# A decoder layer on one core: the end rewritten with a transposed down projection

## The chip, the cores and the metric

The kernel runs on one core of a Trainium2 chip. TensorE multiplies into PSUM (eight banks of 128 x 512 floats), VectorE and ScalarE read PSUM and SBUF, GpSimd reads SBUF alone, and SyncE (SP) only issues transfers. The engines run side by side and wait for each other by semaphores. The metric is the device time of one execution in microseconds (us); less is better.

## The reference

One decoder layer on x (1024 tokens of 128) with a context of 6404 tokens. Three parts, each followed by a residual and a layer norm:

```python
x = _layernorm(x + attn(x, U))                       # softmax of -dist^2 of x @ U
x = _layernorm(x + xattn(ctx, ctx, x, Wq, ..., Wo, bo))   # 16 heads of depth 8, 6404 keys
x = _layernorm(x + ffn(x, clip_x, clip_down, w_gate, w_up, w_down))

def ffn(x, ...):                                     # inner width 352
    xq = act_fake_quant(x, clip_x)      # one scale for the whole tensor:
                                        # sigmoid(clip) * max|x| / 127, round, clip to [-128, 127]
    gate = xq @ weight_fake_quant(w_gate).T          # one scale per row of a weight
    up = xq @ weight_fake_quant(w_up).T
    h = act_fake_quant(silu(gate) * up, clip_down)   # again one scale for the whole tensor
    return h @ weight_fake_quant(w_down).T
```

Both activation scales need the largest value of a whole tensor before the next step can begin.

## The kernel before

Everything is hand-scheduled: every engine has its own program, and the order of its instructions and its waits is written out. Until about 72 us the first attention runs, beside the projection of keys and values and the rounding of the feed-forward weights on VectorE (`ffn_weights`, seven parts between other work). Then comes the loop over `PHASES` = 8 phases (4 groups of heads by 2 halves of the queries) of 17 chunks of 384 keys: TensorE makes scores (line 1404) three banks at a time, ScalarE takes their exponential (line 768), VectorE takes one unit of most chunks over with a polynomial (lines 1055 to 1088, with GpSimd at line 641), and TensorE multiplies by the values (line 1434) into two accumulator banks. In most phases `add_acc`, `turn_acc` and four transfers bring the divided result to `o_t` while the next phase runs. The loop ends at 743.4 us with the last exponentials.

The end is one serial stretch:

- TensorE projects the first half of the queries by `wo_sb` (`project_out(0)`, line 1518), and multiplies the last values. VectorE adds `x1_bo` (line 1120) and takes the statistics (line 834).
- Last phase: VectorE copies and adds the accumulators (lines 1041, 1042), TensorE transposes them (1532), VectorE takes a reciprocal of 16 columns (1129) and multiplies (1131), TensorE turns it back (1551), ScalarE copies it into `o_t` (789), TensorE projects the second half. In between, TensorE transposes the rounded weights (1541, 1546), spreads `dn_diag`, the scale of the down rows (1536), and VectorE copies all that (1138, 1142, 1147).
- Second layer norm: moments (840), square root on ScalarE (803), reciprocal and shift (1153, 1154), five rows of 128 tokens on VectorE (845) and three on ScalarE (797). A tile of "row j" holds 128 tokens by 128 columns.
- First scale: the largest of x2 (1173), transposed into one row (1569), reduced (1165), spread by a matmul with `ones_row` (1571), multiplied by the clip (1168), reciprocal (1170).
- x2 is transposed (1564), scaled and rounded by adding `ROUND` (808, 1178), and clipped into `xq_t` (1180 to 1187).
- Three tiles of the inner width (128, 128, 96 rows), each over all 1024 tokens: gate and up (1584, into four banks), silu on ScalarE (815), product (1195) and its largest value (1200) on VectorE.
- Second scale in the same way, then h is scaled and rounded (VectorE 1206, ScalarE 821) and clipped (1211, 1213) into `hq`.
- Down (1596): `hq` is the stationary operand, 24 matmuls of 128 columns. Its result stands with tokens on the partitions; VectorE multiplies it by the scales (1220), adds x2 (1225), and takes the statistics; then the third norm and two output transfers, five rows by SP (553) and three by ScalarE (828).

`zeros_into` (line 1237) issues matmuls of zeros between the steps. `Chain.step` makes an engine wait for its own instruction. GpSimd has nothing to do in the end.

Of the kernel before, what the change touches and what calls it, by code (L numbers as in the profile page):

```python
# [23 lines left out]
BF16 = mybir.dt.bfloat16  # L24
# [19 lines left out]
G = 4  # L44
# [16 lines left out]
DVE_ROWS = 5  # L61
# [32 lines left out]
def decoder_layer(nc, x, ctx_in, U, Wq, bq, Wk, bk, Wv, bv, Wo, bo, clip_x, clip_down,  # L94
                  w_gate, w_up, w_down, out, score_limit=SCORE_LIMIT):
    stack = ExitStack()
    with stack:
# [20 lines left out]
        ones_row = sb("ones_row", [1, P])  # L118
        minus_sel = sb("minus_sel", [P, 1])
        eps_col = sb("eps_col", [P, 1])  # L120
        round_col = sb("round_col", [P, 1])
        last_rows = sb("last_rows", [P, G])
# [56 lines left out]
        last_rden = sb("last_rden", [P, 4, G])  # L179
        last_att = sb("last_att", [P, 4, G, DH])  # L180
# [14 lines left out]
        dn_diag = sb("dn_diag", [P, D])  # L195
        ones_sq = sb("ones_sq", [P, P])
        dn_bc = sb("dn_bc", [P, D])
        gmax = sb("gmax", [P, 8])
        gmax_row = sb("gmax_row", [1, 2])
        act_s = sb("act_s", [P, 8])  # L200
        gu_s = sb("gu_s", [P, 2, IT])
# [11 lines left out]
        x2_t = attn_e[:, 2 * IT, :]  # L213

# [43 lines left out]
        pe_tail, dve_tail, act_tail = sem("pe_tail"), sem("dve_tail"), sem("act_tail")  # L258
# [173 lines left out]
        def _(sp):  # L432
# [90 lines left out]
            all_written()  # L523
            for ph in range(PHASES):
# [27 lines left out]
            sp.wait_ge(dve_tail, TAIL_OUT)  # L552
            sp.dma_start(out_rows[:, 0:DVE_ROWS, :], res[:, 0:DVE_ROWS, :]).then_inc(out_written, 16)
# [5 lines left out]
        def _(pool):  # L559
# [5 lines left out]
            pool.memset(round_col[:], ROUND)  # L565
            chain.step(pool.memset(last_rows[:], 1.0))
# [20 lines left out]
            pool.memset(v_all[:, :, :, DH:DH + 1], 1.0)  # L587

# [12 lines left out]
            pool.memset(ones_row[:], 1.0)  # L601
# [42 lines left out]
            for ph in range(PHASES):  # L644
                for c in range(NC):
                    m = ph * NC + c
                    stage(m % 2, m, c * CT, ph % NG * G)
                    if c != 1 and c < NC - 1:
                        powers(ph, c)


        @block.scalar
        def _(act):
# [121 lines left out]
            for ph in range(PHASES):  # L775
# [8 lines left out]
                for s in range((NC - 1) * BPC, BPP):  # L784
# [3 lines left out]
            act.wait_ge(pe_tail, TAIL_ATT_T)  # L788
            act.activation(o_t[32 * (NG - 1):P, HQ:T], ps[32 * (NG - 1):P, 1, :], ACT.Copy
                           ).then_inc(act_tail, 1)  # L790
            act.preload_act_table(ACT.Sqrt)

            def norm(signal, target):

                act.wait_ge(dve_tail, signal)
                for j in range(DVE_ROWS, TQ):
                    last = act.activation(target[:, j, :], res[:, j, :], ACT.Identity,
                                          scale=rstd[:, j:j + 1], bias=shift[:, j:j + 1])
                return last


            act.wait_ge(dve_tail, TAIL_VAR2)
            act.activation(rstd[:], mean_var[:, :, 1], ACT.Sqrt, bias=eps_col[:]).then_inc(act_tail, 1)
            norm(TAIL_NORM2, x2).then_inc(act_tail, 1)
            act.preload_act_table(ACT.Silu)

            act.wait_ge(dve_tail, TAIL_S2)
            act.activation(x2_t[:, HQ:T], ps[:, 1, :], ACT.Identity, scale=act_s[:, 1:2],
                           bias=round_col[:]).then_inc(act_tail, 1)
            for rows, a, b in ISPANS:  # L810
                for i in range(a, b):
                    act.wait_ge(pe_tail, TAIL_GU + 2 * i)
                    act.wait_ge(dve_tail, TAIL_XQ)
                    bank = 4 * (i % 2)
                    act.activation(silu[0:rows, i, :], ps[0:rows, bank:bank + 2, :], ACT.Silu,
                                   scale=gu_s[0:rows, 0, i:i + 1]).then_inc(act_tail, 1)
            act.preload_act_table(ACT.Sqrt)

            act.wait_ge(dve_tail, TAIL_S3)
            for rows, i in ((P, 1), (I - 2 * P, 2)):  # L820
                act.activation(h_f[0:rows, i, :], h_f[0:rows, i, :], ACT.Identity,
                               scale=act_s[0:rows, 3:4], bias=round_col[0:rows, :]).then_inc(act_tail, 1)

            act.wait_ge(dve_tail, TAIL_VAR3)
            act.activation(rstd[:], mean_var[:, :, 1], ACT.Sqrt, bias=eps_col[:]).then_inc(act_tail, 1)
            norm(TAIL_NORM3, res).then_inc(act_tail, 1)
            act.wait_ge(act_tail, ACT_OUT)
            act.dma_start(out_rows[:, DVE_ROWS:TQ, :], res[:, DVE_ROWS:TQ, :]).then_inc(out_written, 16)


        def spread(dve, js):

            for j in js:
                last = dve.bn_stats(stats[:, j, :], res[:, j, :])  # L834
            return last

        def moments(dve):

            for j in range(TQ):
                last = dve.bn_aggr(mean_var[:, j, :], stats[:, j, :])  # L840
            return last

        def normalise(dve, target, js):
            for j in js:
                last = dve.tensor_scalar(target[:, j, :], res[:, j, :], mean_var[:, j, 0:1],
                                         rstd[:, j:j + 1], ALU.subtract, ALU.mult)
            return last

        @block.vector
        def _(dve):  # L850
# [52 lines left out]
            def ffn_weights(part):  # L903
# [24 lines left out]
                elif part == 4:  # L928
                    for w, _, q in each:
                        last = dve.tensor_scalar(q, w, ROUND, None, ALU.subtract)  # L930
                    dve.tensor_scalar(dn_diag[:], ident[:], w_dn_s[:, 1:2], None, ALU.mult)
# [712 lines left out]
```

## Time and profile before

| | us |
|---|---|
| runs shown, median (lowest to highest) | 790.36 (789.95 to 790.44) |
| the profiled execution | 790.35 |
| its span | 788.6 |
| busy: PE / ScalarE / VectorE / GpSimd | 702.3 / 723.9 / 602.8 / 176.3 |
| granted TensorE clock, mean of the span | 0.993 |

The profile shows one execution. Its span is from the first to the last recorded event, and the device time has a little around it. Times in the rows are counted from the span's start. A chain of work is followed back from the last instruction, at each step to what released it. The granted clock is 1.00 at 2.4 GHz and 0.50 at 1.2 GHz. A float matmul is recorded as two passes, each with a weight load.

### The profile page before, as it was taken

To read this page: it belongs to the slowest core of one execution; us is meant where nothing else is said; L and a number is where in the kernel's file an instruction comes from. 1 tells how busy PE (TensorE), PEld (TensorE's weight loads), DVE (VectorE), ACT (ScalarE), POOL (GpSimd) and SP (SyncE) were. 2 spreads that over 40 slices of the span, in tenths; PEclk is the share of its full clock that TensorE was granted. 3 is DMA by queue.
4 is the path that set the end of the run, shared out by engine and by line. 5 is a ranking of instruction groups with operands and counts; after the bars stand their busy time and mean duration, and the time that the engine had idled before them with its cause. 6 is when DMAs were issued, how large, how long until landed. Compare 5 with 4: busy or idle time off the path is not lost.

```text
span 788.6 us, 36646 instructions
## 1 busy us (share of the span) xinstructions
PE 702.3 (89%) x15159; PEld 312.5 (40%) x15163; DVE 602.8 (76%) x1709; ACT 723.9 (92%) x632; POOL 176.3 (22%) x318
## 2 busy tenths in 40 slices
PE   9998999989999999989999999899999999899864
PEld 5464344334443344334433443344334443444332
DVE  4668688768886888678867887788868886788676
ACT  4477999999999999999999999999999999999751
POOL 4437122212221222122221222122212221222100
PEclk9999999999999999999999999999999999999997
DMA  4364111111111111111111111111111111111000
GB/s 139 119 178 158 41 45 36 37 44 43 36 37 43 45 39 36 41 44 41 35 40 45 42 35 40 45 42 36 36 45 45 37 36 42 39 34 37 4 1 27
DMA packets 36980, 38.35 MB, mean 49 GB/s; under 512 B 8936, under 2 KB 35466, under 8 KB 36884
## 3 DMA queue, kind: packets, MB, share of 16 engines
q1 hardware_dynamic: 35776, 36.57, 15.9%
q8 instruction: 65, 1.06, 0.5%
q10 hardware_dynamic: 1108, 0.46, 0.2%
q14 instruction: 31, 0.25, 0.1%
HBM read 30.12 MB, written 6.42 MB: 46 GB/s over the span
## 4 chain that ended last, share of the span: by engine, by line
ACT 58%; issue 26%; PE 11%; DVE 3%; ACTq 1%; DVEq 0%
ACT probs L768 57%; PE ps L1311 2%; PE ps L1237 1%; PE ps L1264 1%; PE ps L1272 1%; PE ps L1302 1%; PE ps L1434 1%; PE ps L1255 1%; PE ps L1404 1%; ACTq L781 1%; ACTq L766 0%; DVE stats L834 0%; DVE probs L1195 0%; PE ps L1518 0%; PE ps L1353 0%
## 5 line engine op out<-in xcount | busy, mean ns | idle before, releaser
L768 ACT ACTIVATE probs<-ps 128x1536 f32<-128x1536 f32 (+1 forms) x536 | 669.3, 1393 | 2.0 <-PE ps L1404 2.0
L1434 PE MATMUL ps<-probs,v_op 64*9 64x512 f32 (+1 forms) x8256 | 522.8, 496 | 0.0
L1404 PE MATMUL ps<-q_op,k_op 59*32 59x512 bf16 x6432 | 332.5, 379 | 63.0 <-ACT probs L768 60.7
L1404 PEld LDWEIGHTS ps<-q_op,k_op 59*32 59x32 bf16 x6432 | 101.6, 89 | 347.8 <-issue 259.1
L1055 DVE TENSOR_SCALAR e_t<-ps 128x256 f32<-128x256 f32 x240 | 90.8, 420 | 142.7 <-PE ps L1404 142.7
L1434 PEld LDWEIGHTS ps<-probs,v_op 64*9 64x9 f32 x8256 | 171.3, 86 | 62.2 <-issue 4.2
L641 POOL TENSOR_SCALAR e_pow<-e_t 128x512 int32<-128x512 int16 x120 | 74.3, 619 | 356.0 <-DVE e_t L1055 356.0
L634 POOL COPY v_op<-v_all 128x108 f32<-128x108 f32 x136 | 64.4, 474 | 168.3 <-PE ps L1434 167.8
L1083 DVE SCALAR_TENSOR_TENSOR e_f<-e_f,e_pow 128x256 f32<-128x256 f32 x240 | 98.8, 450 | 0.0
L1077 DVE SCALAR_TENSOR_TENSOR e_f<-e_u,e_f 128x256 f32<-128x256 f32 x240 | 90.6, 419 | 0.0
L1072 DVE SCALAR_TENSOR_TENSOR e_u<-e_f 128x256 f32<-128x256 f32 x240 | 90.3, 418 | 0.2
L1088 DVE SCALAR_TENSOR_TENSOR probs<-e_u,e_f 128x256 f32<-128x256 f32 x240 | 89.7, 412 | 0.0
L1061 DVE SCALAR_TENSOR_TENSOR e_f<-ps,e_t 128x256 f32<-128x256 f32 x240 | 89.6, 415 | 0.0
L704 ACT ACTIVATE probs<-ps,neg_n 128x1024 f32<-128x1024 f32 x8 | 8.9, 1113 | 18.9 <-PE ps L1302 18.9
L1237 PE MATMUL ps<-zeros_bf 128*128 128x512 bf16 x79 | 22.4, 427 | 3.1 <-DVE probs L1195 1.4
L883 DVE SCALAR_TENSOR_TENSOR probs<-ps,bias_cols,k_parts 128x384 f32<-128x384 f32 x17 | 10.5, 616 | 17.7 <-ACT k_parts L690 10.3
L594 POOL TENSOR_TENSOR k_parts<-probs,k_parts 128x384 bf16<-128x384 f32 x17 | 15.5, 912 | 1.4
L1264 PE MATMUL ps<-ctx_t,wk_turned 128*128 128x384 f32 x34 | 14.8, 518 | 0.7 <-DVE probs L883 0.7
L592 POOL CAST k_parts<-probs 128x384 bf16<-128x384 f32 x17 | 8.5, 503 | 30.1 <-DVE probs L883 29.9
L1311 PE MATMUL ps<-probs,x_nat 128*128 128x512 f32 x32 | 15.1, 593 | 0.0
L1272 PEld LDWEIGHTS ps<-wv_sb,ctx_t 128*128 128x128 f32 x102 | 13.6, 191 | 3.4 <-issue 0.5
L1272 PE MATMUL ps<-wv_sb,ctx_t 128*128 128x128 f32 x102 | 14.0, 275 | 0.0
(186 smaller groups left out, 244.9 us busy)
## 6 DMA issues: line engine op xcount, KB each, us to landing
k_op<-k_parts_dram SPq DMA_DIRECT2D x544, 36.0 KB
k_parts_dram<-k_parts SPq DMA_DIRECT2D x17, 288.0 KB, 2.9
k_op<-k_parts_dram SPq DMA_DIRECT2D x272, 12.0 KB
ctx_nat<-in_ctx_dram SPq DMA_DIRECT2D x16, 192.0 KB, 3.2
q_op<-q_parts_dram SPq DMA_DIRECT2D x32, 48.0 KB
q_parts_dram<-q_parts SPq DMA_DIRECT2D x2, 384.0 KB, 3.5
x_nat<-in_x_dram SPq DMA_DIRECT2D x1, 512.0 KB, 3.6
o_t<-att_rows SPq DMA_DIRECT2D x28, 16.0 KB
```

Of the source, the lines that this page charges most:

```text
L634: pool.tensor_copy(v_op[:, slot].rearrange("p j (h d) -> p j h d", h=G), v_all[:, bass.ds(tile, CT), head:head + G, :]).then_inc(v_staged, 1)
L641: pool.tensor_scalar(e_pow[:], e_low(e_t[:]), float(2 ** 23), float(EXP2_LEAD), ALU.mult, ALU.add).then_inc(e_pow_ready, 1)
L768: act.activation(probs[:, b % NP].rearrange("p u t -> p (u t)")[:, 0:columns], ps[:, bank:bank + BU, :].rearrange("p u t -> p (u t)")[:, 0 ...
L1055: dve.tensor_scalar(e_t[:, cols], score, E_MIN, ROUND + EXP2_OFF, ALU.max, ALU.add).then_inc(e_step, 1)
L1061: dve.scalar_tensor_tensor(out=e_f[:, cols], in0=score, scalar=E_MIN, in1=e_low(e_t[:, cols]), op0=ALU.max, op1=ALU.subtract).then_inc(e_s ...
L1072: dve.scalar_tensor_tensor(out=e_u[:, cols], in0=e_f[:, cols], scalar=a, in1=e_f[:, cols], op0=ALU.add, op1=ALU.mult).then_inc(e_step, 1)
L1077: dve.scalar_tensor_tensor(out=e_f[:, cols], in0=e_u[:, cols], scalar=d, in1=e_f[:, cols], op0=ALU.add, op1=ALU.mult).then_inc(e_step, 1)
L1083: dve.scalar_tensor_tensor(out=e_f[:, cols], in0=e_f[:, cols], scalar=e, in1=e_pow[:, cols].bitcast(F32), op0=ALU.add, op1=ALU.mult).then_ ...
L1088: dve.scalar_tensor_tensor(out=probs[:, block % NP, BU - 1, 512 - EW + cols.start:512 - EW + cols.stop], in0=e_u[:, cols], scalar=b, in1=e ...
L1272: last = pe.matmul(ps[:, v_bank(n), P * j:P * j + P], ctx_t[:, n % 3, P * j:P * j + P], wv_sb[:], start=True, stop=True)
L1404: return pe.matmul(ps[a:a + P // G, bank, :], k_op[W2 * r:W2 * r + KR, kslot, i, P * j + a:P * j + a + P // G], q_op[W2 * r:W2 * r + KR, q ...
L1434: last = pe.matmul(ps[32 * k:32 * k + DH + 1, ACC[h], a:b], v_op[W2 * h:W2 * h + W2, slot, j, (DH + 1) * k:(DH + 1) * (k + 1)], probs[W2 * ...
```

## The change

- Entry of the loop: TensorE transposes the rounded weights before it reads the flag; VectorE copies them there (`w_t_made`, `w_t_copied`), and TensorE's second score block waits for that. SP loads rows of Wo into `wo_pad` with four more transfers. GpSimd makes `den_sel`, a matrix that spreads the denominators.
- Last phase: no transposes. ScalarE copies half an accumulator, VectorE adds the other, TensorE spreads the denominators over the partitions with `den_sel`, VectorE takes a reciprocal of [128 x 256] and multiplies, twice. The projection accumulates x1 + bo (`added`), the older heads, and the last ones through `wo_pad`, in PSUM.
- The second norm runs in parts: rows 0 to 3 early, 4 and 5, then 6 and 7, with values read from PSUM.
- The scale: the largest values are put on a diagonal with the clip, a matmul with `ones_sq` spreads them, and one reduce takes the largest.
- Feed-forward: six units of 512 tokens instead of three of 1024; VectorE makes all six products and their largest values. `gu_s` is made by GpSimd.
- Rounding h: tile 0 on VectorE, tile 1 on ScalarE, tile 2 on GpSimd, the clipping mostly on VectorE, in halves.
- Down: the weights are the stationary operand, nine matmuls in three column groups (`DOWN`); the result stands transposed, is scaled into `o_s` per partition, and TensorE turns it back onto x2, which stands in PSUM already.
- The third norm reads PSUM; ScalarE takes rows 0 to 3 and VectorE 4 to 7, with a transfer of 256 KB each.

The diff, cut to its core:

```diff
+            pool.wait_ge(scale_ready, 1)
+            for rows, a, b in ISPANS:
+                pool.tensor_scalar(gu_s[0:rows, :, a:b], w_gu_scale[0:rows, :, a:b],
+                                   act_s[0:rows, 0:1], None, ALU.mult).then_inc(gu_s_ready, 1)
+            pool.wait_ge(scale_ready, 2)
+            rows = FFN_ROWS[2]
+            for half in range(2):
+                cols = slice(HQ * half, HQ * half + HQ)
+                chain.step(pool.tensor_scalar(h_f[0:rows, 2, cols], h_f[0:rows, 2, cols],
+                                              act_s[0:rows, 3:4], ROUND, ALU.mult, ALU.add))
+                pool.tensor_scalar(hq[0:rows, 2, cols], h_f[0:rows, 2, cols], ROUND, QMAX,
+                                   ALU.subtract, ALU.min).then_inc(h_pool, 1)
...
+            for half in range(2):
+                cols = slice(EH * half, EH * half + EH)
+                act.activation(acc_sb[:, cols], ps[:, ACC[0], cols], ACT.Copy).then_inc(acc_copied, 1)
...
+                chain.step(act.activation(h_f[:, 1, cols], h_f[:, 1, cols], ACT.Identity,
+                                          scale=act_s[:, 3:4], bias=round_col[:]))
+                act.activation(hq[:, 1, cols], h_f[:, 1, cols], ACT.Identity, bias=unround_col[:]
+                               ).then_inc(h_act, 1)
...
+            for half, cols in enumerate(halves):
+                dve.wait_ge(den_spread, half + 1)
+                dve.wait_ge(acc_summed, half + 1)
+                chain.step(dve.reciprocal(rden[:, cols], ps[:, half, 0:EH]))
+                dve.tensor_tensor(att[:, cols], acc_sb[:, cols], rden[:, cols], ALU.mult
+                                  ).then_inc(att_scaled, 1)
...
+            def on_diagonal(n, column, clip):
+                dve.tensor_scalar(diag[:, n, :], ident[:], gmax[:, column:column + 1],
+                                  sig[:, clip:clip + 1], ALU.mult, ALU.mult).then_inc(diag_ready, 1)
...
+            for u, (i, half, rows) in enumerate(FFN_UNITS):
+                cols = slice(HQ * half, HQ * half + HQ)
+                dve.wait_ge(gu_done, 2 * u + 2)
+                dve.wait_ge(silu_ready, u + 1)
+                dve.scalar_tensor_tensor(
+                    out=h_f[0:rows, i, cols], in0=ps[0:rows, FFN_BANKS[u][1], :],
+                    scalar=gu_s[0:rows, 1, i:i + 1], in1=silu[0:rows, i, cols],
+                    op0=ALU.mult, op1=ALU.mult).then_inc(h_ready, 1)
+                dve.wait_ge(h_ready, u + 1)
+                last = largest_of(u)
...
             pe.wait_ge(bo_ready, 1)
+            wt = ps[:, 4, :].bitcast(BF16)
...
+            last.then_inc(w_t_made, 1)
             pe.wait_ge(flag_ready, 1)
             with pe.If(pe.value_load(flag[0:1, 0:1]) > 0):
...
+            pe.wait_ge(h_ready, 4)
+            added(0, x2[:, 0:4, :], 4)
+            added(1, x2[:, 4:6, :], 2)
+            added(5, x2[:, 6:8, :], 2)
+            zeros_into(7, 8)
+            spread_max(2, 0)
+            zeros_into(6, 9)
+            for n, (bank, a, b) in enumerate(DOWN):
+                pe.wait_ge(hq_ready, a // HQ + 1)
+                for i, rows in enumerate(FFN_ROWS):
+                    last = pe.matmul(ps[:, bank, 0:b - a], w_dn_t[0:rows, i, :], hq[0:rows, i, a:b],
+                                     start=(i == 0), stop=(i == IT - 1))
+                last.then_inc(down_done, 1)
...
+FFN_UNITS = [(i, half, FFN_ROWS[i]) for half in range(2) for i in range(IT)]
+FFN_BANKS = [(2, 3), (4, 6), (7, 0), (1, 5), (2, 3), (4, 6)]
+DOWN = [(2, 0, HQ), (3, HQ, HQ + EH), (4, HQ + EH, T)]
```

## Rows read from the trace of the kernel before

**Rows 1.** The page, chain that ended last, share of the span by line.
```profile
ACT probs L768 57%; PE ps L1311 2%; PE ps L1237 1%; PE ps L1264 1%; PE ps L1272 1%; PE ps L1302 1%; PE ps L1434 1%; PE ps L1255 1%; PE ps L1404 1%; ACTq L781 1%; ACTq L766 0%; DVE stats L834 0%; DVE probs L1195 0%; PE ps L1518 0%; PE ps L1353 0%
```

**Rows 2.** The chain in order of time, 743 us on: start, us, what.
```profile
743.39 2.73 PE ps L1434 x40
...
759.19 0.76 DVE probs L1178
...
763.39 1.29 DVE probs L1195
...
772.95 0.76 DVE probs L1206
...
777.06 0.87 PE ps L1596 x12
...
779.47 0.87 DVE stats L834 x4
...
782.66 0.65 DVE mean_var L840 x8
...
784.11 1.26 ACT res L797 x3
```

**Rows 3.** Timeline of ScalarE's queue, its last row: start, us, engine, line, operation.
```profile
785.40 0.37 ACTq L828 DMA_DIRECT2D out_dram<-res  x1
```

**Rows 4.** Groups by line and form, ScalarE: count | busy us, mean ns | idle.
```profile
L815 ACT ACTIVATE probs<-ps,gu_s 128x1024 f32<-128x1024 f32 x2 | 2.1, 1111 | 2.2 <-PE ps L1584 2.2
...
L665 ACT ACTIVATE x_t<-ps 128x512 f32<-128x512 f32 x1 | 0.6, 597 | 1.5 <-PE ps L1246 1.5
```

**Rows 5.** Groups by line and form, VectorE, wide operations.
```profile
L1055 DVE TENSOR_SCALAR e_t<-ps 128x256 f32<-128x256 f32 x240 | 90.8, 420 | 142.7 <-PE ps L1404 142.7
...
L1195 DVE SCALAR_TENSOR_TENSOR probs<-ps,gu_s,probs 128x1024 f32<-128x1024 f32 x2 | 2.6, 1280 | 1.9 <-ACT probs L815 1.9
...
L1220 DVE SCALAR_TENSOR_TENSOR res<-ps,act_s,dn_bc 128x512 f32<-128x512 f32 x2 | 1.5, 744 | 1.0 <-PE ps L1596 1.0
...
L992 DVE TENSOR_REDUCE q_abs<-q_parts 128x1 f32<-128x512 bf16 x2 | 1.3, 672 | 0.0
```

**Rows 6.** TensorE: a group by form, and a row of the chain.
```profile
L1311 PE MATMUL ps<-probs,x_nat 128*128 128x512 f32 x32 | 15.1, 593 | 0.0
...
750.75 1.17 PE ps L1518 x8
```

**Rows 7.** Groups by line and form, VectorE, reciprocals.
```profile
L1095 DVE RECIPROCAL att_rden<-acc_t 128x16 f32<-128x16 f32 x7 | 1.8, 254 | 0.2
L1153 DVE RECIPROCAL rstd<-rstd 128x8 f32<-128x8 f32 x2 | 0.4, 203 | 0.4 <-ACT rstd L825 0.4
...
L948 DVE RECIPROCAL attn_rden<-attn_den 128x8 f32<-128x8 f32 x1 | 0.2, 193 | 0.0
```

**Rows 8.** Line 922 on VectorE (ns min/median/max), and GpSimd's timeline at that time.
```profile
L922 DVE TENSOR_SCALAR w_gu<-w_gu,w_gu_inv x6: 273/274/798, 30.0 to 31.5; 128x128 f32<-128x128 f32 x4, 96x128 f32<-96x128 f32 x2
...
29.81 0.91 POOL L594 TENSOR_TENSOR k_parts<-probs,k_parts 128x384 bf16<-128x384 f32 x1
```

**Rows 9.** Groups by line and form, GpSimd, tensor_scalar.
```profile
L641 POOL TENSOR_SCALAR e_pow<-e_t 128x512 int32<-128x512 int16 x120 | 74.3, 619 | 356.0 <-DVE e_t L1055 356.0
...
L574 POOL TENSOR_SCALAR wq_sb<-wq_sb 128x128 f32<-128x128 f32 x1 | 0.5, 522 | 0.0
```

**Rows 10.** Stretches of 1 us: PE, PEld, DVE, ACT, POOL busy (count), PEclk, DMA.
```profile
767.00:768.00 1.00, 0.82 (x2) 0.28 (x3) 0.96 (x2) 0.81 (x1) 0.00 (x0) 0.57 0.00 0
...
770.00:771.00 1.00, 1.00 (x5) 0.35 (x3) 0.96 (x2) 0.00 (x0) 0.00 (x0) 0.72 0.00 0
```

**Rows 11.** Timelines of TensorE, VectorE and SP at the loop's entry.
```profile
73.13 0.61 PE L1404 MATMUL ps<-q_op,k_op 59*32 59x512 bf16 x12 [1.46 <-issue]
...
76.60 0.76 DVE L1055 TENSOR_SCALAR e_t<-ps 128x256 f32<-128x256 f32 x2 [2.99 <-PE ps L1404]
...
79.52 4.71 SPq L331 DMA_DIRECT2D k_op<-k_parts_dram  x6
```

More of the change, by code:

```diff
@@ L833, in spread, with moments @@
+            last.then_inc(out_act, 1)
+            act.wait_ge(out_act, 1)
+            act.dma_start(out_rows[:, 0:HALF, :], res[:, 0:HALF, :]).then_inc(out_written, 16)
+        def spread(dve, tiles):
+            for j, tile in tiles:
+                last = dve.bn_stats(stats[:, j, :], tile)
+            return last
+        def moments(dve, js):
             for j in js:
[L834 to L839, printed above, removed]
@@ L965, in _ @@
             dve.wait_ge(res_ready, 2)
-            chain.step(spread(dve, range(TQ)))
-            moments(dve).then_inc(var_ready, 1)
+            chain.step(spread(dve, res_rows(range(TQ))))
+            moments(dve, range(TQ)).then_inc(var_ready, 1)
             dve.wait_ge(std_ready, 1)
@@ L1227, in _, with inverse @@
-            chain.step(last)
-            moments(dve).then_inc(dve_tail, 1)
-            norm(ACT_STD3, res)
+            dve.wait_ge(res_projected, 1)
+            chain.step(dve.tensor_tensor(res[:, 0:HALF, :].rearrange("p j d -> p (j d)"), ps[:, 2, :],
+                                         x1_bo[:, 0:HALF, :].rearrange("p j d -> p (j d)"), ALU.add))
+            chain.step(spread(dve, res_rows(range(HALF))))
+            moments(dve, range(HALF)).then_inc(ln_var, 1)
+            def inverse(js, std, count):
+                dve.wait_ge(std, count)
+                chain.step(dve.reciprocal(rstd[:, js], rstd[:, js]))
@@ new lines, in _ @@
+            for half, cols in enumerate(halves):
+                dve.wait_ge(den_spread, half + 1)
[3 more added lines that the diff above has]
+                                  ).then_inc(att_scaled, 1)
+            dve.wait_ge(res_projected, 2)
+            chain.step(spread(dve, bank_rows(3, (4, 5))))
+            moments(dve, (4, 5)).then_inc(ln_var, 1)
@@ new lines, in _ @@
+            pe.wait_ge(x1_bo_ready, 1)
+            added(3, x1_bo[:, 4:6, :], 2)
+            added(4, x1_bo[:, 6:8, :], 2)
+            pe.wait_ge(den_sel_ready, 1)
+            for half in range(2):
+                pe.wait_ge(acc_summed, half + 1)
+                pe.matmul(ps[:, half, 0:EH], den_sel[:].rearrange("p k i -> p (k i)"),
+                          acc_sb[:, EH * half:EH * half + EH], start=True, stop=True).then_inc(den_spread, 1)
+            pe.wait_ge(o_written, 16 * G * (PHASES - 1))
@@ new lines, in _ @@
+            pe.wait_ge(wo_pad_loaded, 16 * G)
+            for half in range(2):
+                rows = [(ps[:, 3 + half, P * n:P * n + P], EH * half + P * n) for n in range(2)]
+                for to, a in rows:
+                    pe.matmul(to, o_t[0:D - 32, HQ + a:HQ + a + P], wo_sb[0:D - 32, :], start=False,
+                              stop=False, skip_group_check=True)
+                pe.wait_ge(att_scaled, half + 1)
+                for to, a in rows:
+                    last = pe.matmul(to, att[:, a:a + P], wo_pad[:], start=False, stop=True,
+                                     skip_group_check=True)
+                last.then_inc(res_projected, 1)
@@ L1604 @@
+            turned_back(5, (6, 7))
 W_LOADS = 16 * 5
```

472 lines of the change are left out of this document (251 added, 221 removed).

## The prediction

> **What bounds the kernel now.** I read the page first, and there the chain that ended last: 57% of the span is ScalarE's exponentials [rows 1]. That loop isn't touched, so only two stretches can move: the entry of the loop near 72 us, and the end. The chain in order of time gives the end as one line of steps, each waiting for the one ahead [rows 2]: TensorE's last values end at 746.12, the first activation scale is used at 759.19, the first silu times up starts at 763.39, the second scale is used at 772.95, the down projection starts at 777.06 and the last rows are normalised from 784.11. The output transfer is issued at 785.40 [rows 3]. Of 788.6 us of span, 42.5 us is this serial end, in which no engine is full; its price is the sum of latencies on whichever engine has the baton, mostly VectorE. The profiled execution took 790.35 us, its span 788.6 and 1.75 us around it; the median shown is 790.36, so a shift in the span can be taken from the median directly. 0.2% is 1.6 us, about what a measurement of this kernel can tell from no change.
>
> **The change part by part.** I write the new end out with durations of like instructions, 0.03 us for a hop between engines, and compare at the milestones of [rows 2].
>
> *Attention's last division.* Before: copy, add, four transposes, a 16-wide reciprocal, a multiply, four matmuls, a copy, the projection; the second half of the residual is complete only at 752. New: ScalarE copies 256 columns (0.38 us: 597 ns for 512 [rows 4], less some 0.9 ns a column), VectorE adds 256 (0.42, as the 256-wide PSUM form [rows 5]), TensorE spreads denominators (256 float columns in two passes; a pass of 512 is 15.1/32 = 0.47 [rows 6], so some 0.6 with the latency). It has two `added` matmuls ahead, 0.94, and can start only at 747.0. The reciprocal starts at 747.6. It is now 256 wide, twice. No such width is in the trace. At 8 and 16 columns it took 203 and 254 ns [rows 7], 6.3 ns a further column, while other operations pay about 1 (1280 ns against 744 for 1024 against 512 [rows 5]). Lower bound: 0.42, as any 256-wide operation; upper bound 16 times the 16-wide one, 4.1. I take 254 + 240 x 6.3 = 1.75 us, the slope of the nearest rows. With a 0.42 multiply behind each, both halves are done at 752.0, so this move alone wins nothing.
> The Trainium skill ("VectorE: DVE Perf Modes", the section on the pipe's eight slices) gives the reciprocal an iterative divide with a repeat count of 8. At the 0.96 GHz that the skill gives VectorE that is an estimate of 8.3 ns a column, 2.25 us each, and the sum would be 1.0 us later; the trace's own increments are lower.
>
> *Second layer norm and first scale.* After 752.0 VectorE does stats and moments of rows 4, 5 (0.7: four stats take 0.87, eight moments 0.65 [rows 2]), the largest of half of x2 (0.69, from 672 [rows 5]), a diagonal (0.27), stats and moments of rows 6, 7 (0.7), two tiny ops (0.4), ScalarE two rows (0.87, by three in 1.26 [rows 2]), the other largest (0.69), diagonal (0.27), a spread matmul (0.4), a reduce of 256 (0.42), a reciprocal (0.16), hops 0.3, less 0.3 of overlap. Sum 5.6: the scale is ready at 757.6 against 759.2, gain 1.6. The old route through one row, a matmul and a multiply goes away.
>
> *Quantised x.* The scale to the first half's xq: ScalarE 0.5, VectorE 0.43 and 0.3, with hops 1.4. Then one matmul (0.4), a silu of 512 (0.66: 1111 ns for 1024 [rows 4], less 512 x 0.9), hops: the first silu times up starts at 760.15 against 763.39, gain 3.2. gu_s moved to GpSimd, two tiny ops under 0.6 us of others' work; uncovered they would cost 0.4. The weight copies and the transposes that stood here have left for the loop's entry.
>
> *Six units instead of three.* Before, a unit is 1.28 + 1.22 with overlap, 2.45, three are 7.4. New: 0.75 + 0.69 less 0.05 = 1.39, six are 8.4. Silus and matmuls run ahead, so VectorE sets this; halving costs 1.0. End 768.6 against 770.8, gain 2.1. Maximum 0.15, diagonal 0.27, spread 0.4, reduce 0.28, reciprocal 0.16, hops: scale two at 770.0 against 772.95, gain 2.95.
>
> *Rounding h.* Before, 4.1 us on VectorE. New: ScalarE takes tile 1 (4 ops, 3.1 us), GpSimd tile 2 (4 ops of 96x512), VectorE the rest. If all ran side by side the last would be ready after 3.7. But they don't: a VectorE tensor_scalar of 128x128, 274 ns at the median, took 798 at the worst, the one that started at 30.0, while GpSimd had a tensor_tensor running until 30.72 [rows 8]. I read that as the two alternating on SBUF-to-SBUF work. GpSimd's op isn't in the trace in this form: 0.62 by the int16 one of 512 columns, or 0.52 for only 128 [rows 9], which scaled is 1.5. I take 0.7, nearest to the row of the same width; four of them and VectorE's 3.2 of such work, partly overlapped, give 5.0 (bounds 3.7, and 9.4 in the last rival). Down starts for good at 775.0 against 777.06; the gain falls to 2.05.
> The skill ("GPSIMD Engine Reference", overview table) says the SBUF interface is shared with VectorE's two-port modes and two-input operations. By it the PSUM-sourced steps stay free.
>
> *Down and output.* Before 8.35 from first matmul to issue: 24 matmuls, scaling, adding x2 (two passes of 0.75 + 0.69) and then stats. New: last two groups 0.55, eight passes turning back (1.17, as the eight of [rows 6]), stats 0.87, moments 0.4, stats 0.87, moments 0.4, reciprocal and shift 0.4, four rows on ScalarE 1.65, hops: 6.35. Adding x2 went to TensorE, under VectorE's units. Issue at 781.35 against 785.40, gain 4.05. Two transfers of 256 KB, one issued 0.5 earlier, instead of 320 and 192 KB at once: I take a gain of 0.3 (bounds 0 and 0.6; from issue to the span's end it is 3.2 [rows 3]).
>
> *What is to be paid.* (1) TensorE's clock. Before, it stood at 1.2 GHz from 767.0, after a stretch with one group of four matmuls, and was back during 770 to 771, under zero matmuls [rows 10]. New: between the fourth unit's matmuls (near 761) and the fourth unit's product (765.0) TensorE has two bursts of 0.43, less still. Behind that stand `added` (1.9) and eight zeros (1.8), done at 768.8 at full clock, needed at 769.1. At half clock for most of it they end 1 us late, and the spread matmul is queued behind them. I charge 1.0 there, 0.2 for the thin stretch at 749 to 753, 0.5 for the turning back after 3 us with three matmuls. Bounds 0 and 3.0. (2) The loop's entry. Nine bf16 transposes (eight float passes as wide take 1.17 [rows 6]; bf16 ones less, some 0.8) stand ahead of TensorE's read of the flag; the first scores start at 73.13 after 1.46 us idle, put down to "issue" [rows 11]: the flag's read and its branch. If these start only behind the transposes, the scores are up to 0.8 late; I take 0.55 (bounds 0 and 0.8), and ScalarE's exponentials wait with them. The four VectorE copies (1.0) lie under its 2.99 us of waiting there, and w_t_copied is due only at the second score block. SP's four small DMAs (six loads take 4.71 [rows 11], so some 3) stand ahead of its first load_k at 79.52, but that is for the fifth chunk, four slots ahead: nothing. wo_pad's memset takes the place of dn_diag's multiply, and den_sel's two GpSimd ops lie where GpSimd waits for VectorE's first k part: nothing.
>
> Sum: 4.05 + 0.3 - 1.7 - 0.55 = 2.1 us: 790.35 - 2.1 = 788.3 us.
>
> **The rivals.**
> - *The clock holds or the ports don't collide.* For: nothing else in the end of before ran slow; against: TensorE has less to do there than where it fell. Without the 1.7, 786.6; without the 1.3 of alternating, 787.0; both, 785.3.
> - *A steeper reciprocal.* The fastest 8-wide one (193) and the 16-wide one (254 [rows 7]) give 7.6 ns a column, 2.1 us each: 789.0. This is what the skill's rule on the divide would do here.
> - *GpSimd's op at the dearer rate, half hidden*: 1.5 us each adds 2.5: 790.8.
> - *Ends slower: GpSimd bounds the rounding.* At 1.5 us each and nothing overlapped, 5.9 + 0.2 + 3.3 = 9.4 after the scale instead of 5.0: 792.7. It loses against before as soon as rounding takes over 7.1 us, and by 0.2% from 8.7.
> - *The six units don't flow*: if each silu waited for the product before it, 2.1 a unit, 4.3 more: 792.6. Against it: banks are free for the first four.
>
> **How the numbers follow.** Forecast 0.42 (787.0 to 789.6; above 788.8 for a quarter of it), first rival 0.20, steep reciprocal 0.13 (half again under 788.8, less a little), half-hidden GpSimd 0.12, the two slow ones 0.13, of which 0.03 would end within 0.2%. Faster by over 0.2%: 0.32 + 0.20 + 0.06 = 0.58; within: 0.32; slower: 0.10. The range leaves the tip of the first rival and the slow cases out: 785.4 to 790.9.
>
> **What would show it.** The two 256-wide reciprocals: about 1.75 us each right, 0.4 or over 2 wrong. The clock at half between the fourth product and the second scale. GpSimd's and VectorE's durations between the scale and down: h's rounding over 3.7 us with ops stretched by each other. Six units in 8.4 us. First scores near 73.7. The forecast is wrong if the stretch from the last values to the output's issue isn't near 37 us (39.3 before), or if the loop itself has a different length.

## The result, and the profile after

The changed kernel takes 792.05 us (median; 791.71 to 794.16). The kernel before, run beside it on the same chip, takes 790.36. The ratio is 1.0025 with a 95% interval of 1.0016 to 1.0033: slower by 1.7 us, a small loss but clear of the noise. The forecast was 788.3 with a range of 785.4 to 790.9, so it was wrong, in its sign as well.

The profiled execution took 792.24 us, its span 790.5, 1.9 more than before. First the chain in order of time, answering [rows 2] (start, us, what):

```profile
743.49 2.72 PE ps L1556 x40
...
747.93 1.77 DVE probs L1222
...
750.07 1.76 DVE probs L1222
...
758.32 0.57 ACT probs L860
...
758.94 0.40 issue
759.34 0.44 DVE xq_t L1268
...
761.46 0.76 DVE probs L1283
...
765.61 0.75 DVE probs L1283
...
766.40 3.62 PE ps L1652 x6
770.02 1.78 PE ps L1346 x8
771.81 0.23 PE ps L1685 x2
...
772.65 0.99 POOL probs L683
773.64 0.08 issue
773.72 1.98 POOL k_parts L685
...
775.80 0.75 POOL dn_s L688
776.54 0.82 POOL probs L683
...
779.42 0.30 DVE k_parts L1312
...
779.76 1.46 PE ps L1719 x6
781.22 1.72 PE ps L1726 x8
```

Down to the products of the feed-forward the new end is ahead of the old one: the first stands at 761.46 against 763.39, the second scale is used at 772.6 against 772.95. Then GpSimd, which had nothing to do in the old end, is on the chain with its four operations on tile 2 (lines 683 and 685). A fifth stands between its two halves: the 128 x 1 product that makes `dn_s`, the scale of the down projection (line 688). It takes 0.75 us, and neither the core of the diff nor the prediction has it. The down projection starts for good at 779.76, where the old one started at 777.06. The output transfer, 785.40 before [rows 3], now is (timeline of ScalarE's queue):

```profile
787.40 0.35 ACTq L893 DMA_DIRECT2D out_dram<-res  x1
```

The rounding of h, from the timelines of VectorE and GpSimd (start, us, engine, line, operation, in brackets the idle time before and what ended it):

```profile
773.11 0.80 DVE L1302 TENSOR_SCALAR k_parts<-probs 128x512 bf16<-128x512 f32 x1
773.72 1.98 POOL L685 TENSOR_SCALAR k_parts<-probs 96x512 bf16<-96x512 f32 x1
773.95 0.57 DVE L1304 TENSOR_SCALAR k_parts<-k_parts 128x512 bf16<-128x512 bf16 x1
...
774.95 0.29 DVE L1309 TENSOR_SCALAR k_parts<-k_parts 128x512 bf16<-128x512 bf16 x1
...
775.95 0.42 DVE L1302 TENSOR_SCALAR k_parts<-probs 128x512 bf16<-128x512 f32 x1
776.40 0.29 DVE L1304 TENSOR_SCALAR k_parts<-k_parts 128x512 bf16<-128x512 bf16 x1
...
776.52 0.85 POOL L683 TENSOR_SCALAR probs<-probs,act_s 96x512 f32<-96x512 f32 x1
777.45 1.93 POOL L685 TENSOR_SCALAR k_parts<-probs 96x512 bf16<-96x512 f32 x1
779.42 0.29 DVE L1312 TENSOR_SCALAR k_parts<-k_parts 96x512 bf16<-96x512 bf16 x1 [2.52 <-POOL k_parts L685]
```

Two things are to be seen. Two of VectorE's operations take twice as long while GpSimd works (0.80 and 0.57, against 0.42 and 0.29 for the same lines later). Not all do: the one at 774.95 lies wholly beside GpSimd's 1.98 us and takes 0.29, and what decides it is open. And GpSimd's second operation takes 1.93 us even at 777.45, when VectorE stands idle for 2.52 us waiting for it. So work side by side slows some of VectorE's operations, but it isn't what makes GpSimd's second operation slow.

The clock, in stretches of 1 us, answering [rows 10] (busy time and count of PE, PEld, DVE, ACT, POOL, then PEclk):

```profile
753.00:754.00 1.00, 0.90 (x6) 0.50 (x4) 0.96 (x3) 0.29 (x1) 0.00 (x0) 0.50 0.00 0
...
767.00:768.00 1.00, 1.00 (x2) 0.34 (x1) 0.97 (x3) 0.00 (x0) 0.00 (x0) 0.50 0.06 16
...
777.00:778.00 1.00, 0.00 (x0) 0.00 (x0) 0.00 (x0) 0.69 (x1) 0.91 (x2) 0.50 0.00 0
...
780.00:781.00 1.00, 1.00 (x6) 0.73 (x5) 0.00 (x0) 0.38 (x1) 0.00 (x0) 0.50 0.00 0
```

Before, the clock was at 1.2 GHz once while the chain needed TensorE; now it is three times: 753 to 756.4, 766.6 to 770, and 777 to 783.7, each time after a stretch in which TensorE had little to do. The last covers the whole down projection and the turning back.

### The profile page after: what moved, and what is told of

It is laid out like the page before. It is cut to its first block, busy times and chain, and to the rows that moved or that the text cites. A ratio compares the mean times of both kernels' runs of the same rounds, so it can differ in the third digit from the quotient of the medians.

```text
span 790.5 us, 36671 instructions
## 1 busy us (share of the span) xinstructions
PE 706.2 (89%) x15149; PEld 315.6 (40%) x15149; DVE 605.5 (77%) x1716; ACT 728.7 (92%) x648; POOL 183.9 (23%) x327
## 3 DMA queue, kind: packets, MB, share of 16 engines
q8 instruction: 65, 1.06, 0.5%
## 4 chain that ended last, share of the span: by engine, by line
ACT 57%; issue 26%; PE 11%; DVE 3%; ACTq 1%; POOL 1%; POOLq 0%; DVEq 0%
ACT probs L808 56%; PE ps L1420 2%; PE ps L1373 1%; PE ps L1381 1%; PE ps L1346 1%; PE ps L1411 1%; PE ps L1556 1%; PE ps L1364 1%; ACTq L821 1%; PE ps L1652 1%; DVE probs L1222 0%; ACTq L806 0%; PE ps L1526 0%; DVE probs L1283 0%; DVE stats L899 0%
## 5 line engine op out<-in xcount | busy, mean ns | idle before, releaser
L1346 PE MATMUL ps<-zeros_bf 128*128 128x512 bf16 x60 | 17.7, 433 | 1.3 <-DVE zeros_bf L925 1.3
```

## The experiments

Their lines are counted in their own files, so the same step has another number in some of them. Except where said, an experiment is the changed kernel with one edit.

**1. Tile 2 of h rounded by VectorE.** GpSimd keeps only the small scale `dn_s`, which it now makes first.

```diff
-                chain.step(pool.tensor_scalar(h_f[0:rows, 2, cols], h_f[0:rows, 2, cols],
-                                              act_s[0:rows, 3:4], ROUND, ALU.mult, ALU.add))
-                pool.tensor_scalar(hq[0:rows, 2, cols], h_f[0:rows, 2, cols], ROUND, QMAX,
-                                   ALU.subtract, ALU.min).then_inc(h_pool, 1)
...
+                rounded(0, half)
+                chain.step(rounded(2, half))
+                lowered(0, half)
+                chain.step(lowered(2, half))
```

> The changed kernel with GpSimd's four operations on tile 2 of h given to VectorE; nothing left out. Theory A (GpSimd's own operations bound the rounding: 7.2 us from the second scale to the last matmuls' start in the changed kernel, 1.93 us for one subtract-and-min of 96x512 even while VectorE rests): VectorE needs about 5.0 us for all, so the time falls by about 2.2 us, from 792.0 to 789.8. Theory B (the loss is TensorE at 1.2 GHz, and the rounding is only late because everything is): the rounding takes as long as before, and the time stays within 0.5 us of 792.0.

Measured: 790.13 us (787.9 to 791.7), ratio to before 0.9998 (0.9989 to 1.0008), so 1.9 us less than the changed kernel; the two intervals don't touch. The last group's down projection starts at 777.40, 4.8 after the scale instead of 7.2:

```profile
775.86 0.76 DVE L1294 TENSOR_SCALAR k_parts<-probs 128x512 bf16<-128x512 f32 x2
...
777.40 1.46 PE L1711 MATMUL ps<-k_parts,w_dn_t 128*128 128x256 bf16 x6 [1.49 <-DVE k_parts L1311]
```

VectorE makes one such operation in 0.38 us here, and rounds both tiles within the 4.8 us. The six matmuls still take 1.46: the clock is at 0.50 there too. GpSimd's part in the loss is shown; it is not all of it. This run takes the slow operations and `dn_s` off the chain together, so it doesn't tell them apart; number 5 does.

**2. GpSimd without the `min`.** VectorE takes it over in its clipping.

```diff
-                pool.tensor_scalar(hq[0:rows, 2, cols], h_f[0:rows, 2, cols], ROUND, QMAX,
-                                   ALU.subtract, ALU.min).then_inc(h_pool, 1)
+                pool.tensor_scalar(hq[0:rows, 2, cols], h_f[0:rows, 2, cols], ROUND, None,
+                                   ALU.subtract).then_inc(h_pool, 1)
```

> The changed kernel with the min taken out of GpSimd's second operation (it subtracts alone, and VectorE's clip of that tile does min and max in one, as it does for tile 1). Theory A1 (the min, or the second operation, is what costs 1.93 us on GpSimd): that line falls to 0.6 to 0.9 us, rounding ends after about 5.1 us instead of 7.2, time about 789.9. Theory A2 (GpSimd is slow because VectorE's operations hold its way to SBUF, or the bf16 output is slow): the line stays near 1.9 us and the time near 792.0.

Measured: 792.02 us, ratio 1.0022 (1.0012 to 1.0032), as slow as the changed kernel. In the trace (of an execution of 791.13) the operation fell from 1.98 and 1.93 to:

```profile
773.67 1.66 POOL L685 TENSOR_SCALAR k_parts<-probs 96x512 bf16<-96x512 f32 x1
...
777.09 1.50 POOL L685 TENSOR_SCALAR k_parts<-probs 96x512 bf16<-96x512 f32 x1
```

The `min` is worth some 0.4 us each time; 1.5 is left for a bare `subtract`. The rounding got 0.7 us shorter in the trace (6.5 for 7.2) and the median didn't move; why not, no run shows. The operation neither fell to 0.6 to 0.9 nor stayed near 1.9, so neither theory fits. It left open whether the bf16 output or the operation is dear.

**3. The zeros ahead of the products by x2.** `zeros_into(7, 8)` is moved from behind `added` to after the third product.

```diff
+            pe.wait_ge(h_ready, 3)
+            zeros_into(7, 8)
             pe.wait_ge(h_ready, 4)
             added(0, x2[:, 0:4, :], 4)
             added(1, x2[:, 4:6, :], 2)
             added(5, x2[:, 6:8, :], 2)
-            zeros_into(7, 8)
```

> The changed kernel with the eight zero matmuls that stood between `added` and the spread of the second maximum moved ahead of `added`, into TensorE's pause after the sixth unit. Theory: the spread no longer queues behind them (it started at 771.64 in the changed kernel, 1.25 us after its input at 770.38), so the second scale comes 1.2 us earlier and the time is about 790.8. If the clock still falls the zeros and `added` run at 1.2 GHz, about 5.5 us from 765.0, and the gain is gone but for 1.2 - 0.1. Rival (it is the clock alone, not the queue, that costs): less than 0.3 us.

Measured: 791.75 us, ratio 1.0015 (1.0005 to 1.0025), 0.3 less than the changed kernel, and the intervals overlap: the 1.2 us expected didn't come. The queue ahead of the spread is gone; it starts as soon as its diagonal is there, and in the middle of the end the clock stands. The spread, in TensorE's timeline:

```profile
771.14 0.49 PE L1685 MATMUL ps<-diag,ones_sq 128*128 128x128 f32 x2 [1.80 <-DVE diag L1235]
```

But TensorE was slow at both ends (stretches of 5, 4 and 6 us; the third column from the end is PEclk):

```profile
752.00:757.00 5.00, 4.37 (x15) 3.23 (x17) 4.56 (x18) 2.57 (x5) 0.00 (x0) 0.50 0.00 0
766.00:770.00 4.00, 3.35 (x14) 1.67 (x12) 3.90 (x7) 0.85 (x1) 0.00 (x0) 1.00 0.02 4
777.00:783.00 6.00, 3.78 (x21) 3.33 (x21) 1.20 (x5) 1.16 (x2) 1.93 (x1) 0.54 0.00 0
```

The spread now follows its diagonal at once, where it was 1.25 us late in the changed kernel; but it starts only 0.5 us earlier than there (771.14 against 771.64), since the first low stretch was longer (752 to 758.6 for 753 to 756.4) and had made all ahead of it later: the first product stands at 762.16, against 761.46. Mending this one pause alone brings little.

**4. Copies instead of the two wide reciprocals.** This kernel leaves the last division out.

```diff
-                chain.step(dve.reciprocal(rden[:, cols], ps[:, half, 0:EH]))
+                chain.step(dve.tensor_copy(rden[:, cols], ps[:, half, 0:EH]))
```

> The changed kernel with its two 256-wide reciprocals replaced by copies of the same width; this leaves the division of the last phase out. Theory (both lie on the path, 1.76 us each against 0.41 for a copy): 2.7 us less, 789.3. Rival (something else, the clock or the largest values, bounds that stretch): less than 1 us.

Measured: 789.92 us (788.32 to 791.59), ratio 0.9999 (0.999 to 1.0009). The copy takes 0.42, and the gate matmuls start at 757.45 instead of 760.15, 2.7 us earlier:

```profile
747.80 0.42 DVE L1222 COPY probs<-ps 128x256 f32<-128x256 f32 x1 [0.52 <-PE ps L1662]
...
757.45 1.90 PE L1707 MATMUL ps<-xq_t,w_gu_t 128*128 128x512 bf16 x8 [0.80 <-DVE xq_t L1270]
```

So the two reciprocals of 1.76 us lie wholly on the chain. The median gained 2.1 us. The span of the profiled execution is 3.9 us shorter than the changed kernel's, but that execution is the fastest of its ten: in it the clock doesn't fall before 775.5, and the second spread follows its diagonal at once too.

**5. GpSimd with `mult` and `add`.** Same tile, same output type, same number of operands as the changed kernel's second operation: only the pair of operations is another. VectorE takes the `min` over in its clipping, as in 2.

```diff
-                pool.tensor_scalar(hq[0:rows, 2, cols], h_f[0:rows, 2, cols], ROUND, QMAX,
-                                   ALU.subtract, ALU.min).then_inc(h_pool, 1)
+                pool.tensor_scalar(hq[0:rows, 2, cols], h_f[0:rows, 2, cols], 1.0, -ROUND,
+                                   ALU.mult, ALU.add).then_inc(h_pool, 1)
```

> The changed kernel with GpSimd's second operation on tile 2 written as times 1.0, plus -ROUND (the same values) instead of subtract and min; VectorE's clip of that tile does min and max in one. Same engine, same shape, same bf16 output. Theory A3 (the pair of operations sets GpSimd's price: mult and add took 0.62 to 0.98 us for 512 columns, subtract with min 1.93, subtract alone 1.50): the line falls to 0.6 to 0.95 us, the rounding to about 5.0 us, the time to about 790.0. Rival (the bf16 output or the input left in a bad place makes it slow): the line stays at 1.5 us, the time above 791.

Measured: 789.85 us (787.53 to 791.07), ratio 0.9992 (0.9983 to 1.0002). The operation:

```profile
773.28 0.66 POOL L685 TENSOR_SCALAR k_parts<-probs 96x512 bf16<-96x512 f32 x1
...
775.13 1.06 POOL L685 TENSOR_SCALAR k_parts<-probs 96x512 bf16<-96x512 f32 x1
...
776.79 0.83 PE L1719 MATMUL ps<-k_parts,w_dn_t 128*128 128x256 bf16 x6 [0.53 <-DVE k_parts L1312]
```

That settles it: neither the bf16 output nor the width, but the operations. The last matmuls start 4.7 us after the second scale, inside the forecast's 5.0, with `dn_s` (0.60 here) still between GpSimd's halves. On 96 x 512 GpSimd takes 0.66 to 1.06 for `mult, add`, 1.50 to 1.66 for `subtract` alone, 1.93 to 1.98 for `subtract, min`. The median gained 2.2 us, what two operations at 1.95 - 0.86 = 1.1 us less each make. The profiled execution is 2.1 us below its median (787.76 against 789.85) and its clock falls once only before 782 (751.4 to 758.3), so its span isn't to be set against the median. It shows one thing more: with the clock at 2.4 GHz between 758.3 and 782, `added` and the eight zeros, still ahead of the second spread, are done before the diagonal is.

```profile
771.10 0.49 PE L1685 MATMUL ps<-diag,ones_sq 128*128 128x128 f32 x2 [0.33 <-DVE diag L1235]
```

TensorE waits 0.33 us for the diagonal here, where the changed kernel's spread came 1.25 us after it. So the queue alone costs nothing at that place; the queue at 1.2 GHz does.

**6 to 8. TensorE kept busy.** Zeros ahead of each half of the last projection, after the third product (as in 3), more of them behind the second spread, and some after the first down group. With GpSimd as in the changed kernel (6), as in 5 (7), and with VectorE rounding as in 1 (8). The counts are those of 8; 6 has 16 and 12 in the last two places, 7 has 13 and 7.

```diff
+                zeros_into(5, 5 if half == 0 else 4)
                 pe.wait_ge(att_scaled, half + 1)
...
-            zeros_into(6, 9)
+            zeros_into(6, 11)
...
                 last.then_inc(down_done, 1)
+                if n == 0:
+                    zeros_into(6, 7)
```

> The changed kernel with zero matmuls in TensorE's pauses: five and four beside the two reciprocals, the eight ahead of `added`, sixteen instead of nine after the second spread and twelve after the first group of the down projection. Theory (three falls to 1.2 GHz cost 0.5, 1.2 and 1.4 us on the path): the clock stays at 2.4 GHz through the end and the time is about 789.0. Rival (the falls lie where TensorE isn't on the path, and GpSimd's lateness alone is what counts): above 791.0.

> Both mends at once (the pauses filled, GpSimd's second operation as times 1.0 plus -ROUND). If the two costs are separate they add: about 787.0, and faster than the kernel before by 0.4%. If they hide each other: not below 788.5.

> The pauses filled and tile 2 rounded by VectorE instead of GpSimd. The VectorE version's rounding took 4.7 us, so about 786.8; if filling the pauses gives nothing it stays at the 790.1 of the VectorE version alone.

Measured: 789.92 (ratio 0.9991, 0.9981 to 1.0), 788.18 (0.9972, 0.9961 to 0.9982) and 787.47 (0.9963, 0.9948 to 0.9977). Number 8, the same three stretches:

```profile
752.00:757.00 5.00, 3.46 (x20) 2.04 (x19) 4.52 (x18) 2.63 (x5) 0.00 (x0) 1.00 0.00 0
766.00:770.00 4.00, 2.53 (x10) 1.33 (x8) 3.83 (x8) 0.03 (x1) 0.00 (x0) 1.00 0.01 4
777.00:783.00 6.00, 1.78 (x16) 1.59 (x15) 4.68 (x24) 2.23 (x7) 0.00 (x0) 1.00 0.00 0
```

and its timelines of TensorE and of ScalarE's queue:

```profile
776.16 0.84 PE L1713 MATMUL ps<-k_parts,w_dn_t 128*128 128x256 bf16 x6
...
782.25 0.35 ACTq L885 DMA_DIRECT2D out_dram<-res  x1
```

The same six matmuls take 0.84 instead of 1.46, and from them to the transfer's issue it is 6.1 us instead of 7.64. Filling alone gives 2.1 (6 against the changed kernel), the rounding on VectorE alone 1.9 (1), both together 4.6 (8): they add, and the 0.5 over is inside the intervals. All three came out 0.7 to 1.2 us above what was expected (789.0, 787.0, 786.8). In 6 one stretch at 1.2 GHz was left, from 765.2 to 768.6, under the early zeros; its spread starts at 770.39, number 8's at 770.33, so it cost nothing.

**9 to 11. A narrow reciprocal, and the scales on VectorE.** 9 is number 8 with TensorE turning the denominators so that 8 columns hold a half's. Both halves are inverted there, copied out 32 times a column, and spread by four matmuls with `ident`; the filling zeros go into another bank. 10 is number 8 with `gu_s` made by VectorE. 11 is both.

```diff
-                chain.step(dve.reciprocal(rden[:, cols], ps[:, half, 0:EH]))
-                dve.tensor_tensor(att[:, cols], acc_sb[:, cols], rden[:, cols], ALU.mult
+                chain.step(dve.reciprocal(last_rden[:, 2 * half:2 * half + 2, :],
+                                          ps[:, half, 0:2 * G].rearrange("p (j k) -> p j k", k=G)))
...
+                dve.tensor_copy(rden_wide[:, 2 * half:2 * half + 2].rearrange("p j k i -> p (j k) i"),
+                                bass.AP(r.tensor, r.offset, [list(r.ap[0]), [1, 2 * G], [0, 32]])
...
+                dve.tensor_tensor(att[:, cols], acc_sb[:, cols], ps[:, 2 if half else 5, 0:EH], ALU.mult
```

```diff
-            for rows, a, b in ISPANS:
-                pool.tensor_scalar(gu_s[0:rows, :, a:b], w_gu_scale[0:rows, :, a:b],
-                                   act_s[0:rows, 0:1], None, ALU.mult).then_inc(gu_s_ready, 1)
...
+                if half == 0:
+                    for rows, a, b in ISPANS:
+                        dve.tensor_scalar(gu_s[0:rows, :, a:b], w_gu_scale[0:rows, :, a:b],
+                                          act_s[0:rows, 0:1], None, ALU.mult).then_inc(gu_s_ready, 1)
```

> The kernel with TensorE kept busy and the rounding on VectorE (787.47 us), with one more edit: the denominators of a half are turned by TensorE so that 8 columns hold them, inverted there, copied out 32 times each by VectorE and spread again by TensorE. Theory (the reciprocal's time goes with its columns, 1.75 us for 256, and the chain of the two halves pays two of them): one of 8 columns and the copy should take about 0.2 + 0.4 us in place of 1.75, so two halves lose some 2.3 us of VectorE and gain two short trips to TensorE of about 0.3 us each; the product is done 1.5 to 2 us earlier and the kernel takes 785.5 to 786. Rival (the chain pays for each hand-over between the engines, and each small operation has a floor): the four extra hand-overs eat the gain, and it stays at 787.0 to 787.5.

> The same kernel (787.47 us) with the gate and up scales made by VectorE, after it has made the first half of the codes, in place of GpSimd. Theory (the pause of about 0.45 us that stands ahead of VectorE's second half of the codes is GpSimd's small multiplication lying on the same memory port at that moment): the pause goes, a multiplication of under 0.1 us comes in its place, and the kernel takes about 787.1. Rival (the pause is the wait for ScalarE's own part and its signal): it stays where it is, and the kernel takes 787.4 to 787.6.

> Both edits together, the narrow reciprocal and the scales made by VectorE. If both theories hold their gains add, since they lie one behind the other on the chain: 785.1 us. If only the narrow reciprocal gains it takes what that kernel takes, within 0.2 us.

Measured: 786.02 (785.96 to 786.19; ratio 0.9941, 0.9925 to 0.9956), 787.28 (0.9956, 0.9941 to 0.9971) and 785.88 (785.69 to 786.01; 0.9939, 0.9925 to 0.9952). Number 9, timeline of VectorE:

```profile
748.14 0.21 DVE L1216 RECIPROCAL last_rden<-ps 128x8 f32<-128x8 f32 x1 [0.43 <-PE ps L1666]
748.38 0.29 DVE L1219 COPY rden_wide<-last_rden 128x256 f32<-128x256 f32 x1
...
749.48 0.87 DVE L1225 TENSOR_TENSOR probs<-acc_sb,ps 128x256 f32<-128x256 f32 x2 [0.36 <-PE ps L1672]
751.25 0.50 DVE L894 BATCH_NORM_STATS2 stats<-ps 128x6 f32<-128x128 f32 x2 [0.90 <-PE ps L1686]
```

The second product is done at 750.35, 1.8 us before number 8's 752.17, as the theory has it, although the loop of this execution ended 0.4 us later. Half of that is lost at once: VectorE then waits 0.90 us for the projection, which stands in TensorE's queue behind the older heads' matmuls and two of the zeros that fill the pause. 1.1 us of span and 1.45 of the median are left. In number 10 the pause of 0.54 us ahead of the rounded x stays where it was:

```profile
759.33 0.43 DVE L1256 TENSOR_SCALAR xq_t<-probs 128x512 bf16<-128x512 f32 x1 [0.54 <-ACT probs L848]
```

GpSimd isn't its cause: that theory falls. Its rival, the wait for ScalarE's part, is neither shown nor refuted. In numbers 9 and 11, with more instructions in VectorE's program ahead of this place, the pause behind ScalarE is gone and one of 0.27 us stands one operation earlier:

```profile
757.62 0.48 DVE L1265 TENSOR_SCALAR probs<-ps,act_s 128x256 f32<-128x256 f32 x1 [0.27 <-DVE act_s L1259]
```

The waits in the program are the same, but in 9 VectorE starts 0.24 us behind ScalarE, which is done at 757.94 (757.38 + 0.56), 0.16 before VectorE comes to wait for it. So this can be a pause that goes with the place in the program, or the first pause hides the second; what it is stays open. Numbers 10 and 11 differ from 8 and 9 by less than 0.2 us, which can't be told from nothing. The narrow reciprocal's gain is clear: in the same comparison 9 takes 785.96 to 786.19 and 10, without it, 787.05 to 787.39. Number 9 (and 11) beats both kernels, by 4.6 us against before.

## Why the prediction was wrong

By its own steps, from milestone to milestone of the profiled execution:

| step | predicted | measured | off by |
|---|---|---|---|
| entry of the loop | 0.55 | 0.1 | -0.45 |
| last values to both halves divided | 5.9 | 6.07 | +0.2 |
| to the first scale | 5.6 + 0.2 | 6.0 | +0.2 |
| to the first product | 2.55 | 3.17 | +0.6 |
| six units | 8.4 | 8.39 | 0 |
| to the second scale | 1.4 + 1.0 | 2.7 | +0.3 |
| rounding h | 5.0 | 7.2 | +2.2 |
| down projection to the issue | 6.35 + 0.5 | 7.64 | +0.8 |
| issue to the end | 2.9 | 3.1 | +0.2 |
| sum | | | +4.0 |

The forecast for the span was 786.5 and it came to 790.5.

**The rounding of h** is the step that failed, and it alone takes the forecast's gain of 2.1. The mechanism was named, the size was wrong: "I take 0.7, nearest to the row of the same width". I priced an operation that the trace didn't show by its width, from [rows 9], and both candidates there were other operations (619 ns for 512 columns is a `mult, add`, 522 for 128 a lone `mult`). GpSimd's first operation, a `mult, add` too, took 0.98 and 0.85, its second, `subtract, min`, 1.98 and 1.93: 5.7 us for four that I had at 2.8. A term was left out as well: "four of them", and `dn_s` stands between them with 0.75 us, priced at nothing. Of the stretch on GpSimd (772.65 to 779.4) it is one ninth. Experiment 5 shows that the pair of operations sets the second one's price: with the cheap pair, and `dn_s` where it was, the rounding takes 4.7. Experiment 1 shows that the median gives 1.9 us back when GpSimd's work on the tile is out of it. The upper bound, 1.5 us each, had the right mean by luck, (0.98 + 0.85 + 1.98 + 1.93) / 4 = 1.4: none of the four took 1.5. The case "dearer rate, half hidden", rounding of 7.5, is what came, and the point from which the slower rival was to decide, "over 7.1 us", is where 7.2 lies. I gave the one 0.12 and the slow ones together 0.13. The alternating of the two engines, from [rows 8], was right in part: 0.80 against 0.42, but 0.29 at 774.95.

By itself the 2.2 us makes 790.5, still inside the range. What carried the time out of it are the clock at the down projection (0.8 for that step) and the small steps; the entry of the loop, at 0.1 instead of 0.55, gave 0.45 back. The stretch from the last values to the issue, which was to be "near 37 us", measured 41.2 (746.21 to 787.40).

**The clock** cost more than the 1.7 that I charged, 2.8 in the profiled execution, inside the bounds of 0 and 3.0. At the second scale the diagonal is ready at 770.38 and its spread starts at 771.64, behind `added` and eight zeros, as predicted: 1.25 for 1.0. The fall near 753 cost the chain nothing in this execution: the first scale's second diagonal is ready at 757.08 and spread at 757.13. In that of experiment 3, where it lasted to 758.6, the same spread came at 757.69, 0.5 us behind its diagonal. The one at the down projection was the mis-sized one, 1.54 against 0.5 by experiment 8. I took 3 us with three matmuls there; with GpSimd late it was 5.8 us with three matmuls (773.96 to 779.76), and at 1.2 GHz from 777 to 783.7. So a part of this miss follows from the first one, yet in experiment 1, where the rounding is short, the six matmuls still take 1.46.

**The first product** came 0.6 late for its step, of which 0.40 is the "issue" at 758.94 that no run explains.

**The entry of the loop** was over-charged. The nine transposes are done at 72.13, and the first scores start at 73.04, against 73.13 before [rows 11]:

```profile
73.04 0.61 PE L1526 MATMUL ps<-q_op,k_op 59*32 59x512 bf16 x12 [0.90 <-issue]
```

The idle time put down to "issue" shrank from 1.46 to 0.90: the read of the flag and its branch went on beside the transposes, and the lower bound of 0 was the right end. The scores came at 73.04 for the 73.7 of the forecast. From VectorE's writing of the flag (71.47 before, 71.45 now) to the first scores it is 1.66 us before and 1.59 now. The last values end 0.09 later than before.

**Right were** the reciprocal (1.76 and 1.75 for the 1.75 from [rows 7]) and the six units (8.39 for 8.4). The reciprocal's increment is (1755 - 254) / 240 = 6.3 ns a column. The Trainium skill's repeat count of 8 ("VectorE: DVE Perf Modes", the section on the pipe's eight slices) had given an estimate of 2.25 us; the trace doesn't agree with that as a price, and the measurement decides. (The steep rival's 2.1 us came from [rows 7], 7.6 ns a column, and isn't that estimate.) The output transfer's gain of 0.3 came to 0.1.

**The range** was too narrow, as I see it, for one reason: I took each small term at its likeliest and let only the named cases move it. The terms of the small steps missed in one direction (0.2 + 0.2 + 0.6 + 0.3 + 0.2 = 1.5 us), and a time is late whenever any of them is.

## What to carry to other kernels

Price an operation on an idle engine by the same operation in a trace, not by one of the same width, and if there is none, take the dear bound and ask who would wait for it: work moved to a free engine must be off the chain by the whole width between its bounds. A serial end that gives TensorE less to do can lose part of its gain again at 1.2 GHz, in a pause, so cut the work and fill the pauses in one step, and look at where the filling stands in the queue. A wide reciprocal goes by its columns: turn the values so that they lie in few columns, if TensorE is free.

## What was not expected of the hardware

- GpSimd's tensor_scalar on 96 x 512, bf16 out: 0.66 to 1.06 us for `mult, add`, 1.50 to 1.66 for `subtract`, 1.93 to 1.98 for `subtract, min`; VectorE made the same `subtract, min` in 0.38. The Trainium skill ("GPSIMD Engine Reference", § 4.1 Engine selection) calls one-input work on GpSimd roughly line-rate; against VectorE's 0.38, for the first pair it is a factor of about two, for the last one of five, and the measurement decides.
- Three of the kernels whose pauses aren't filled differ from execution to execution by 3 to 4 us (787.9 to 791.7 in experiment 1, 788.32 to 791.59 in 4, 787.53 to 791.07 in 5), while experiment 3, which shows falls too, keeps within 0.8. Where the low stretch lies differs as well: 751.4 to 758.3 in the profiled execution of 5, 753 to 756.4 in that of 1. With all pauses filled the spread is 0.8 us and less (0.5 in experiments 7 and 8, 0.2 in 9; 8 and 9 have five and four executions only), though a fall is left in some (765.3 to 768.7 in that of 10). The mean granted clock goes the same way in 5 (0.998 at 787.53, 0.990 at 791.07), but not one to one: 787.76 and 789.91 both have 0.993. That the clock makes the spread is likely by this, not shown; but a single trace of the first kind can't stand for its median (787.76 against 789.85 in 5).
- A pause on VectorE of some 0.46 us behind ScalarE's part that is gone, with one of 0.27 us an operation earlier, when its program is longer ahead of it. The cause is open.
